# Attention outputs of a graph layer: the key-value matrix as the stationary operand, query features as the moving one in rounded and rest parts

## The reference

```python
def _apply_kernel(x, orf):
    m, d_k = orf.shape
    proj = jnp.einsum('bhld,md->bhlm', x, orf) / d_k ** 0.25
    norm = jnp.sum(x * x, axis=-1, keepdims=True) / (2.0 * math.sqrt(d_k))
    return (jnp.exp(proj - norm) + EPS) / math.sqrt(m)
...
q_phi = _apply_kernel(q, orf)
k_phi = _apply_kernel(k, orf)
kv = jnp.einsum('bhlm,bhld->bhmd', k_phi, v)
ksum = jnp.sum(k_phi, axis=2)
num = jnp.einsum('bhlm,bhmd->bhld', q_phi, kv)
den = jnp.einsum('bhlm,bhm->bhl', q_phi, ksum)
out = num / den[..., None]
out = out.transpose(0, 2, 1, 3).reshape(B, L, D)
return out @ Wo.T + bo
```

## Time and profile before

| what | us |
|---|---|
| median of three runs (lowest, highest) | 1444.85 (1444.17, 1446.24) |
| time of the profiled execution | 1449.3 |
| its span, first to last instruction | 1447.7 |
| PE busy in the span | 1359.6 (94%) |
| VectorE (DVE) busy | 790.5 (55%) |
| ScalarE (ACT) busy | 563.6 (39%) |
| GpSimd (POOL) busy | 395.8 (27%) |

### The profile page before, as it was taken

One profiled execution on the slowest core, in us unless ns is written; L12 is line 12 of the kernel. 1 busy time (PEld: TensorE's weight loads), 2 busy tenths in 40 slices (PEclk: granted clock), 3 DMA queues, 4 the chain that ended last, 5 costly groups with the idle time before them and its releaser, 6 DMA issues.

```text
span 1447.7 us, 25316 instructions
## 1 busy us (share of the span) xinstructions
PE 1359.6 (94%) x8199; PEld 1201.9 (83%) x8234; DVE 790.5 (55%) x1648; ACT 563.6 (39%) x943; POOL 395.8 (27%) x407
## 2 busy tenths in 40 slices
PE   5899999999989999999999999998999599999996
PEld 2476677899989999999999999987888588888885
DVE  7866444446355656565656565655454634444641
ACT  7322232211044544545454555553222224444541
POOL 7532543244330001010101010003223133333432
PEclk9899999999998999999999999999999599999998
DMA  4111211264410000000000000003245467777853
GB/s 167 49 30 37 66 48 59 77 193 147 119 35 14 30 14 20 24 18 26 16 27 14 29 14 29 0 30 112 57 153 174 172 190 222 219 214 212 275 143 56
DMA packets 58101, 127.78 MB, mean 88 GB/s; under 512 B 7626, under 2 KB 28826, under 8 KB 58048
## 3 DMA queue, kind: packets, MB, share of 16 engines
q1 hardware_dynamic: 48016, 96.79, 20.3%
q0 software_dynamic: 10032, 30.30, 8.6%
HBM read 91.46 MB, written 37.43 MB: 89 GB/s over the span
## 4 chain that ended last, share of the span: by engine, by line
PE 81%; DVE 8%; issue 4%; ACT 3%; DMA 2%; POOL 1%; DVEq 1%; POOLq 0%; SPq 0%; ACTq 0%
PE PB L1757 7%; PE PB L1759 7%; PE PB L1758 7%; PE PB L1663 7%; PE PB L1973 6%; PE PB L1974 6%; PE PB L1976 6%; PE PB L1795 5%; PE PB L1818 4%; PE PB L1742 3%; PE PB L1743 2%; PE PB L1702 2%; PE PB L1744 2%; PE PB L1703 2%; PE PB L1704 2%
## 5 line engine op out<-in xcount | busy, mean ns | idle before, releaser
L1757 PE MATMUL PB<-xh,hw 128*128 128x416 f32 (+1 forms) x576 | 205.6, 357 | 0.0
L1759 PE MATMUL PB<-xh,hw 128*128 128x416 f32 (+1 forms) x576 | 204.5, 355 | 0.0
L1758 PE MATMUL PB<-xl,hw 128*128 128x416 f32 (+1 forms) x576 | 204.4, 355 | 0.0
L1973 PE MATMUL PB<-mwh,mth 128*128 128x512 f32 x368 | 148.5, 404 | 0.6 <-issue 0.6
L1974 PE MATMUL PB<-mwl,mth 128*128 128x512 f32 x368 | 144.2, 392 | 0.0
L724 POOL CAST hw<-hraw 128x1024 fp32r<-128x1024 f32 x24 | 25.0, 1040 | 429.2 <-DVE qphi L1333 207.1
L1663 PE MATMUL PB<-ohs,ohd 128*128 128x512 bf16 (+1 forms) x530 | 114.4, 359 | 16.7 <-DVE ohs L1209 14.4
L1663 PEld LDWEIGHTS PB<-ohs,ohd 128*128 128x128 bf16 x564 | 49.2, 101 | 80.4 <-DVE ohs L1209 43.9
L1209 DVE TENSOR_SCALAR ohs<-iota,sc 128x1280 bf16<-128x1280 f16 x188 | 113.9, 606 | 0.0
L1976 PE MATMUL PB<-mwh,mtl 128*128 128x512 f32 x368 | 113.9, 391 | 0.0
L1757 PEld LDWEIGHTS PB<-xh,hw 128*128 128x128 f32 x576 | 109.9, 191 | 1.4
(11 more groups left out here) (303 smaller groups left out, 3080.4 us busy)
## 6 DMA issues: line engine op xcount, KB each, us to landing
mraw<-expert_w SPq DMA_DIRECT2D x64, 512.0 KB, 9.1
count_rests<-ATf POOLq DMA_DIRECT2D x9, 640.0 KB, 3.5
xrow<-x SPq DMA_DIRECT2D x40, 128.0 KB, 2.9
y_scratch<-xrow SPq DMA_DIRECT2D x40, 128.0 KB, 2.1
yrow<-y_scratch SPq DMA_DIRECT2D x20, 256.0 KB, 3.0
x2n_half<-xhat SPq DMA_DIRECT2D x20, 256.0 KB, 2.3
out<-x SPq DMA_DIRECT2D x9, 512.0 KB
ATf<-wg SPq DMA_DIRECT2D x32, 128.0 KB, 2.3
```

Source lines behind the costliest of these rows:

```text
L1757: mm(bank(i, n), hw[:, wi, 0, k, :], xh[:, k, c0:c0 + n], start=(k == 0), stop=False)
L1758: mm(bank(i, n), hw[:, wi, 0, k, :], xl[:, k, c0:c0 + n], start=False, stop=False)
L1759: ins = mm(bank(i, n), hw[:, wi, 1, k, :], xh[:, k, c0:c0 + n], start=False, stop=(k == KT - 1))
L1973: mm(y[c], mth[:, k, :], mwh[par][:, k, c * CW:(c + 1) * CW], start=(k == 0), stop=False)
```

## The change: features move, the matrix stands

The key-value matrix becomes the stationary operand, 128 features by 128 columns: 64 value columns, and beside them the sum of the features copied 64 times (`kvh`, and its rest `kvl`). The query features move, rounded (`qh`) and rest (`ql`), a third of the nodes at a time, in three fp32r products for each half of the features. The result has channels on the partitions: 64 partitions of numerators and 64 of denominators. VectorE takes the reciprocals of the denominators straight into `attnT` and multiplies by the numerators in place, so that `att`, `turn` and `keep_turned` go.

ScalarE makes `qh` with one more activation after each `query_exp`, which adds the epsilon; VectorE makes `ql` (`query_low`) where it added the epsilon. `qh` lies on `kphi` and `ql` on `qexp`, so `qh` waits until the key features of the pair are used up, and the next pair's `key_exp` and `values` wait for all outputs of this one. `kvh` serves both heads in turn: `keep_products(1)` now waits for the last output of head 0. Some small tiles (`sums`, `negmean`, `ssq`) move, and GpSimd waits for the first half of the output weights before it splits the second.

```diff
...
-        qphi = keep("qphi", [P, MH, NP], F32, pb)
-        vT = qphi[:, 0, :]
-        kphi = keep("kphi", [P, TT, M], F32, pb)
-        att = kphi[:, :, 0:P]
+        ps = ExitStack()
+        qexp = keep("qexp", [P, MH, NP], F32, ps)
+        vT = qexp[:, 0, :]
+        kphi = keep("kphi", [P, TT, M], F32, ps)
+        ps.close()
+        ql = keep("ql", [P, MH, NP], F32R, pb)
+        qh = keep("qh", [P, MH, NP], F32R, pb)
...
-        kvs = keep("kvs", [P, 2, MH, DK + 1], F32, pa)
+        kvh = keep("kvh", [P, MH, 2 * DK], F32R, pa)
+        kvl = keep("kvl", [P, MH, 2 * DK], F32R, pa)
...
-                if h == 0:
-                    act.wait_ge(aux_done, START + 12 * j + TURNED[i])
+                act.wait_ge(aux_done, START + 10 * j)
...
+                act.wait_ge(aux_done, START + 10 * j)
                 act.wait_ge(proj_done, 6 + 9 * j + 3 + i + 1)
...
                 c0, n = THIRDS[i // 2]
-                act.wait_ge(aux_done, START + 12 * j + 4 + 2 * h)
+                act.wait_ge(aux_done, START + 10 * j + 4 + (i // 2 + 1 if h else 0))
                 act.wait_ge(phi_done, START + 22 * j + f + 1)
-                a.activation(qphi[:, i % 2, c0:c0 + n], bank(3 + f % 2, n), ACT.Exp,
+                a.activation(qexp[:, i % 2, c0:c0 + n], bank(3 + f % 2, n), ACT.Exp,
                              scale=PHI_SCALE).then_inc(exp_done, 1)
+                act.wait_ge(exp_done, 2 + 22 * j + f + 1)
+                act.wait_ge(kv_done, START + 2 * j + 2)
+                a.activation(qh[:, i % 2, c0:c0 + n], qexp[:, i % 2, c0:c0 + n], ACT.Identity,
+                             bias=eps[:, :]).then_inc(qh_ready, 1)
 
...
-            def query_eps(j, h, i):
+            def query_low(j, h, i):
                 c0, n = THIRDS[i // 2]
-                dve.wait_ge(exp_done, 2 + 22 * j + 10 + 6 * h + i + 1)
-                v.tensor_scalar(qphi[:, i % 2, c0:c0 + n], qphi[:, i % 2, c0:c0 + n], EPS_PHI, None,
-                                ALU.add).then_inc(qph_ready, 1)
+                dve.wait_ge(qh_ready, 12 * j + 6 * h + i + 1)
+                v.scalar_tensor_tensor(out=ql[:, i % 2, c0:c0 + n], in0=qexp[:, i % 2, c0:c0 + n], scalar=EPS_PHI,
+                                       in1=qh[:, i % 2, c0:c0 + n].bitcast(F32), op0=ALU.add,
+                                       op1=ALU.subtract).then_inc(qph_ready, 1)
                 def keep_products(h):
-                    dve.wait_ge(aux_done, START + 12 * j)
+                    both_ = bank(5, MH * (DK + 1)).rearrange("p (m d) -> p m d", m=MH)
+                    sums_ = both_[:, :, DK:DK + 1].broadcast_to([P, MH, DK])
+                    vals, dens = slice(DK * h, DK * h + DK), slice(DK - DK * h, 2 * DK - DK * h)
+                    dve.wait_ge(aux_done, START + 10 * j + 7 * h)
                     dve.wait_ge(kv_done, START + 2 * j + h + 1)
-                    v.tensor_copy(kvs[:, h, :, :], bank(5, MH * (DK + 1)).rearrange("p (m d) -> p m d", m=MH)).then_inc(kv_evac, 1)
+                    v.tensor_copy(kvh[:, :, vals], both_[:, :, 0:DK])
+                    v.tensor_copy(kvh[:, :, dens], sums_).then_inc(kv_high, 1)
+                    dve.wait_ge(kv_high, 2 * j + h + 1)
+                    v.tensor_tensor(kvl[:, :, vals], both_[:, :, 0:DK], kvh[:, :, vals].bitcast(F32), ALU.subtract)
+                    v.tensor_tensor(kvl[:, :, dens], sums_, kvh[:, :, dens].bitcast(F32), ALU.subtract).then_inc(kv_evac, 1)
 
                 def keep_outputs(h, i):
-                    f = 4 + 2 * h + i
-                    half = bank(6 + f % 2, 5 * (DK + 1)).rearrange("p (t d) -> p t d", t=5)
-                    dve.wait_ge(aux_done, START + 12 * j + f + 1)
-                    dve.wait_ge(aux_evac, 2 + 12 * j + f)
-                    v.reciprocal(rec[:, :], half[:, :, DK:DK + 1].rearrange("p t a -> p (t a)")).then_inc(rec_done, 1)
-                    dve.wait_ge(rec_done, 4 * j + 2 * h + i + 1)
-                    v.tensor_tensor(att[:, 5 * i:5 * i + 5, DK * h:DK * h + DK], half[:, :, 0:DK],
-                                    rec[:, :].rearrange("p (t a) -> p t a", a=1).broadcast_to([P, 5, DK]),
-                                    ALU.mult).then_inc(aux_evac, 1)
-
-                def keep_turned(i):
-                    t0, nt = VALUE_TILES[i]
-                    dve.wait_ge(aux_done, START + 12 * j + 8 + i + 1)
-                    v.tensor_copy(attnT[:, ds(j, 1), t0 * P:(t0 + nt) * P].rearrange("p a n -> p (a n)"),
-                                  bank(6 + i % 2, nt * P)).then_inc(aux_evac, 1)
+                    f = 4 + 3 * h + i
+                    c0, n = THIRDS[i]
+                    vals, dens = slice(DK * h, DK * h + DK), slice(DK - DK * h, 2 * DK - DK * h)
+                    to = attnT[vals, ds(j, 1), c0:c0 + n].rearrange("p a n -> p (a n)")
+                    dve.wait_ge(aux_done, START + 10 * j + f + 1)
+                    v.reciprocal(to, bank(6 + f % 2, n)[dens, :]).then_inc(rec_done, 1)
+                    dve.wait_ge(rec_done, 6 * j + 3 * h + i + 1)
+                    v.tensor_tensor(to, bank(6 + f % 2, n)[vals, :], to, ALU.mult).then_inc(aux_evac, 1)
...
-                keep_products(1)
-                for i in range(6):
-                    query_eps(j, 0, i)
+                for i in range(4):
+                    query_low(j, 0, i)
                 keep_outputs(0, 0)
+                for i in range(4, 6):
+                    query_low(j, 0, i)
+                keep_outputs(0, 1)
                 if not last:
                     stack_lows(j + 1, 0)
                 else:
                     for k in range(2):
                         low_slab(k)
-                keep_outputs(0, 1)
-                if last:
+                keep_outputs(0, 2)
+                keep_products(1)
+                for i in range(2):
+                    query_low(j, 1, i)
+                if not last:
+                    stack_squares(j + 1, 0)
+                else:
                     for k in range(2, 4):
                         low_slab(k)
-                for i in range(2):
-                    query_eps(j, 1, i)
-                if not last:
-                    stack_squares(j + 1, 0)
-                query_eps(j, 1, 2)
+                for i in range(2, 4):
+                    query_low(j, 1, i)
                 if not last:
                     stack_rests(j + 1, 0)
-                for i in range(3, 6):
-                    query_eps(j, 1, i)
+                keep_outputs(1, 0)
+                for i in range(4, 6):
+                    query_low(j, 1, i)
                 if not last:
                     stack_lows(j + 1, 1)
-                keep_outputs(1, 0)
+                keep_outputs(1, 1)
                 if not last:
                     stack_squares(j + 1, 1)
                     stack_rests(j + 1, 1)
                 else:
                     for k in range(4, 6):
                         low_slab(k)
-                keep_outputs(1, 1)
+                keep_outputs(1, 2)
                 if not last:
                     stack_lows(j + 1, 2)
-                keep_turned(0)
-                keep_turned(1)
...
                 def outputs(h, i):
 
-                    f = 4 + 2 * h + i
-                    pe.wait_ge(aux_evac, 12 * j + f + 1)
-                    pe.wait_ge(qph_ready, 12 * j + 6 * h + (4 if i == 0 else 6))
-                    for q in range(5):
-                        t = 5 * i + q
-                        for m in range(MH):
-                            ins = mm(bank(6 + f % 2)[:, q * (DK + 1):(q + 1) * (DK + 1)],
-                                     qphi[:, m, t * P:(t + 1) * P], kvs[:, h, m, :], start=(m == 0), stop=(m == MH - 1))
+                    f = 4 + 3 * h + i
+                    c0, n = THIRDS[i]
+                    pe.wait_ge(aux_evac, 10 * j + f + 1)
+                    pe.wait_ge(kv_evac, START + 2 * j + h + 1)
+                    pe.wait_ge(qph_ready, 12 * j + 6 * h + 2 * i + 2)
+                    o = bank(6 + f % 2, n)
+                    for m in range(MH):
+                        mm(o, kvh[:, m, :], qh[:, m, c0:c0 + n], start=(m == 0), stop=False)
+                        mm(o, kvl[:, m, :], qh[:, m, c0:c0 + n], start=False, stop=False)
+                        ins = mm(o, kvh[:, m, :], ql[:, m, c0:c0 + n], start=False, stop=(m == MH - 1))
                     ins.then_inc(aux_done, 1)
 
-                def turn(i):
-
-                    t0, nt = VALUE_TILES[i]
-                    pe.wait_ge(aux_evac, 12 * j + 8 + i + 1)
-                    for q in range(nt):
-                        ins = nc.tensor.transpose(bank(6 + i % 2)[:, q * P:(q + 1) * P], att[:, t0 + q, :], ident[:, :])
-                    ins.then_inc(aux_done, 1)
+                def around_first(k):
+                    if k % 4 == 2:
+                        query_features(0, 2 + k // 4)
+
+                def around_second(k):
+                    if k % 4 == 2:
```

(58 more changed lines are left out.)

13 lines of the change are left out of this document (3 added, 10 removed).

## The result

The changed kernel takes 1534.12 us (median of 4 runs, 1532.95 to 1538.14) against 1445.53 us before (4 runs, 1444.17 to 1446.24): ratio 1.0619, 95% interval 1.0597 to 1.0641. The forecast was 1521 us in 1451 to 1556. Its profiled execution took 1538.14 us, 88.8 more than that of before.

| stretch | before | after | difference | forecast |
|---|---|---|---|---|
| start to the first query features | 457.5 | 455.4 | -2.1 | 0 |
| seven steps from pair to pair | 512.0 | 587.0 | +75.0 | +62.7 |
| last pair, to the first row tile | 25.9 | 40.8 | +14.9 | +13.8 |
| first row tile to the end | 453.9 | 455.0 | +1.1 | 0 |

What follows compares the result with a forecast made beforehand. PE bounded the kernel before; VectorE's path with long reciprocals would set the new loop. Seven steps 51.5, last pair 13.8 and clock 11.2 sum to 76.5 on 1449.3: 1525.8, less 4.45 for the median: 1521 us, range 1451 to 1556.

Steps and rivals of the forecast that it cites:

- last pair: End of the attention: VectorE's queued query_low, six reciprocals with products and weight subtractions run up to 1008.4, +13.8 us.
- R: Time of one new VectorE reciprocal of 416 elements a partition: 2.5 us, ends 0.6 and 3.4.
- fixed-extra rival: VectorE's reciprocal has a fixed extra and 2.6 ns an element, 1.3 us each: 1469 us in all, chance 0.15.
- the estimate after the Trainium skill: VectorE's reciprocal as eight steps of 0.96 GHz an element: 3.6 us each, 1558 us in all.
- the clock: PE stands some 8 us a pair, mostly ahead of the key-value products; 3.3 us dips in about half of seven pairs: +11.
- VectorE's part: From VectorE's first subtraction to the end of the last value copies, without pause: 34.8 us a pair without GpSimd's delay.
- the block: GpSimd's first weight split, held up by VectorE's next four key_eps: 2.6 us a pair, between 0 and 3.5.
- the part behind: From VectorE's last value copies to the next pair's query features, PE's work: 22.4 us a pair, unchanged.
- PE's relief: Cheaper outputs and ten fewer transposes on PE: 2.8 us a pair, 22 in all.
- ScalarE's wait: PE stands 2.6 us a pair before head 1's query piece for an exponential behind ScalarE's copies and squares, 2.1 more.
- rival R = 0.6: VectorE's reciprocal at the pace of other operations, 0.6 us: +0 to +1 a pair, 1451 us, chance 0.15.
- The faster rival: Reciprocals of 0.6 us, no delay by GpSimd's split, ScalarE early enough: PE keeps its 22 us gain, 1423, chance 0.05.

Runs made afterwards that it cites:

- the later split: The changed kernel with GpSimd's first split block of a pair started four key-feature sums later: 1506.72 us, ratio 1.0386 to the kernel before.
- the version without the long division: The changed kernel with one later 128x416 reciprocal for both heads, two exponentials of head 1 earlier and GpSimd's block later: 1444.96 us, ratio 1.0002.
- the run without it: The changed kernel with the first two query exponentials of head 1 ahead of ScalarE's copies and squares: 1548.32 us, ratio 1.0706.
- the run with 0.59 us: The changed kernel with each reciprocal replaced by a VectorE operation of the same shape that writes a constant: 1465.61 us, ratio 1.0108.

## Why the prediction was right, point by point

- **What decides: right.** The prediction put 34 reciprocals on the path. The chain of the whole profile has exactly 34 of its line, 94.1 us, 2.77 each. Taking them away moved the time by that price; doubling them moved it by that price and by what the others cost that then came onto the path.
- **R: mis-sized by a tenth.** The mis-sized term is the fit through 5 and 10 elements: 2.5 forecast, 2.76 measured; 34 x 0.26 = 8.8 us of the miss. The elements cost (2.76 - 0.15)/416 = 6.3 ns each, between the slopes 5.2 and 7.8. The fixed-extra rival (1.3) and the pace of other operations (0.6) are out. So is the estimate after the Trainium skill ("VectorE: DVE Perf Modes", "First, the fixed hardware budget"): 8.3 ns by its repeat count of 8.
- **The split and the clock: right kinds, wrong sizes, in opposite directions.** The forecast had 18.2 for the block in seven pairs and 11.2 for the clock (3.3 in half of seven pairs would be 11.5). VectorE's part, where the block stands, took 7.5 more than the sum without it (seven times 34.8); the part behind, where the clock falls, took 27.6 more than seven times 22.4; the first part 0.7 less. So the block was priced at about twice its size (the later split took 10.0 off VectorE's part) and the clock at less than half, and that the total misses by only 5.0 (34.4 against 29.4) is luck. The prediction added the two as if they were separate, with a dip in half of the pairs. The part behind took 25.7 to 27.3 in six of seven steps; in the last one, without a block beside the key stage, it took 22.5. But with the later split alone four of seven steps still had the dip there, so the block is one cause of it and not the only one.
- **The last pair: right.** Forecast 13.8, with the measured R 15.4, measured 14.9. With the small rests of the table (-1.0) the terms close: 8.8 + 5.0 - 0.5 - 1.0 = 12.3, as 88.8 - 76.5.
- **PE's relief and ScalarE's wait: right.** 2.8 a pair forecast, 2.4 measured (71.35 to 68.94, in the version without the long division); the wait 2.6 forecast, 2.7 measured. Beside the long path it does not matter: the chain does not hold it, and the run without it won nothing.
- **The rival R = 0.6 was too low.** It gave 1451; the run with 0.59 us gave 1465.6. "+0 to +1 a pair" was 0.8 to 1.4 in five steps, and it left out clock dips of 3 to 5 us in the other two; the last pair cost 4.0, not 2.4.
- **The faster rival** named what was needed (a division that costs VectorE's path little, exponentials early, no block). With these the time is 1445, and with the end rearranged 1434, not 1423: steady pairs keep 2.8 us in which PE is not busy.

## What to carry to other kernels

Price a reciprocal by its elements per partition: going from 5 sums a partition to 416 copies of sums in one operation is a change of engine load, not of form. Where it must be long, take it off the chain that starts the next stage, let it serve all 128 partitions, and run it where its engine waits for PE. And before adding up a blocked operation and a lost clock, ask whether one causes the other. A test that doubles a cost can bring more onto the path than was there, so look at the chain again. And when an end is pulled forward, look which loads still wait for the old end.

## What was not expected of the hardware

- The reciprocal's time did not grow with the number of partitions: 64x416 from PSUM took 2.76 us, 128x416 from SBUF 2.75, so both heads in one cost half.
- Sixteen useless matmuls a pair took 24.2 us off seven steps (587.0 to 562.8), though they only fill pauses of PE. The pauses of 1.9 and 1.45 us in a pair cost less than the lower clock after them, which made the part behind 27.2 us instead of 22.5.
- A logarithm and an exponential of ScalarE in turn cost 2 x 1283 ns of table loads for 1.07 us of work.
